# Two attention layers on eight cores: row sums by VectorE transposes, bf16 shift, and a first projection stage in four banks

## The reference

```python
qkv = x @ Wqkv.T + b          # first block: 16 query heads, ONE key head and ONE value head of 128
attn = softmax(causal(q k^T / sqrt(128)));  ctx = attn @ v
x = layernorm(x + ctx @ Wout.T + bo)
# second block: 16 heads, each with its own query, key and value, from x @ (Wa * column scale);
# causal attention inside each sequence, then ctx @ Wp
x = layernorm(x + attention2(x))
```

## Time and profile before

| | us |
|---|---|
| median of 3 runs (2007.41 to 2011.96) | 2007.47 |
| the profiled execution, its own time | 2012.48 |
| its span, on core 4, the slowest | 2010.7 |
| spans of the eight cores | 2000.0 to 2010.7 |

### The profile page before, as it was taken

How to read it: one execution, slowest core, us unless ns; L and a number is a source line. 1 busy time by engine, 2 the same in 40 slices (tenths; PEclk the granted TensorE clock), 3 DMA queues, 4 the chain that set the end, 5 groups by cost and what they waited for, 6 DMA issues and landing times.

```text
span 2010.7 us, 31172 instructions; the slowest of 8 cores (2000.0 to 2010.7 us)
## 1 busy us (share of the span) xinstructions
PE 1941.8 (97%) x10704; PEld 1032.5 (51%) x10704; DVE 1097.6 (55%) x1872; ACT 1002.4 (50%) x1395; POOL 242.1 (12%) x354
## 2 busy tenths in 40 slices
PE   5999999999999999999999999999999999899997
PEld 3455455545444444645647465564745647444443
DVE  0088889988953554134555545555555555543433
ACT  0288888888843433144454544545354453532221
POOL 1011111111132441000010000001000000100000
PEclk9999999999999999999999999999999999999999
DMA  9511221221486996132121322212131210393752
GB/s 156 108 33 43 53 59 39 62 50 36 89 169 126 277 262 168 32 53 48 33 53 27 64 43 53 44 37 52 29 64 43 53 37 13 63 213 109 221 186 84
DMA packets 87577, 170.11 MB, mean 85 GB/s; under 512 B 38160, under 2 KB 54912, under 8 KB 77440
## 3 DMA queue, kind: packets, MB, share of 16 engines
q0 software_dynamic: 26304, 59.77, 18.7%
q1 hardware_dynamic: 60976, 107.83, 17.8%
q10 hardware_dynamic: 144, 0.52, 0.1%
HBM read 185.69 MB, written 33.80 MB: 109 GB/s over the span
## 4 chain that ended last, share of the span: by engine, by line
PE 89%; DMA 5%; DVE 2%; ACT 2%; issue 1%; POOL 0%; DVEq 0%; ACTq 0%; POOLq 0%; SPq 0%
PE pj L303 33%; PE c_ps L609 11%; PE s_ps L418 11%; PE s_ps L841 10%; PE pj L1039 10%; PE pj L841 5%; PE l_ps L530 3%; PE c_ps L841 3%; DMA bufB<-wo 2%; PE l_ps L841 2%; DMA bufB<-xT 2%; ACT pt L430 1%; PE pj L383 1%; PE pj L759 1%; PE pj L397 0%
## 5 line engine op out<-in xcount | busy, mean ns | idle before, releaser
L430 ACT ACTIVATE pt<-s_ps,mbias 128x1024 bf16<-128x1024 f32 (+2 forms) x640 | 631.2, 989 | 458.6 <-PE s_ps L418 357.8
L303 PE MATMUL pj<-bufA,ws 128*128 128x512 bf16 x2048 | 480.5, 379 | 2.6 <-DVE ws L965 1.7
L609 PE MATMUL c_ps<-pt,v 128*128 128x512 bf16 (+3 forms) x1280 | 342.3, 349 | 9.2 <-ACT cf L622 8.2
L303 PEld LDWEIGHTS pj<-bufA,ws 128*128 128x128 bf16 x2048 | 198.5, 98 | 232.1 <-issue 5.6
L487 DVE TENSOR_TENSOR acc<-acc,pt 128x1024 f32<-128x1024 f32 x180 | 220.1, 1223 | 123.1 <-ACT pt L430 119.3
L303 PE MATMUL pj<-bufB,ws 128*128 128x512 bf16 x1024 | 275.5, 382 | 1.2 <-DVE mhat L387 0.7
L1039 PE MATMUL pj<-wv,bufA 128*128 128x256 bf16 x2048 | 238.9, 273 | 1.7 <-DVE mbias L400 1.0
L438 POOL TENSOR_SCALAR_AFFINE_SELECT pt<-pt 128x256 bf16<-128x256 bf16 x256 | 123.0, 482 | 905.1 <-ACT pt L430 890.7
L1039 PEld LDWEIGHTS pj<-wv,bufA 128*128 128x128 bf16 x2048 | 199.7, 98 | 39.2 <-issue 2.3
L869 ACT ACTIVATE sqs<-z 128x512 f32<-128x512 f32 x128 | 80.6, 629 | 240.2 <-DVE z L864 231.6
L609 PEld LDWEIGHTS c_ps<-pt,v 128*128 128x128 bf16 x1280 | 124.7, 98 | 144.4 <-issue 21.8
(11 more groups left out here) (113 smaller groups left out, 1879.8 us busy)
## 6 DMA issues: line engine op xcount, KB each, us to landing
rb<-rr_res SPq DMA_DIRECT2D x116, 256.0 KB, 3.5
ws<-wqk POOLq DMA_DIRECT2D x32, 512.0 KB, 5.2
z<-x SPq DMA_DIRECT2D x16, 1024.0 KB, 6.6
x_res<-z SPq DMA_DIRECT2D x16, 1024.0 KB, 6.9
z<-x_res SPq DMA_DIRECT2D x16, 1024.0 KB, 6.6
out<-z SPq DMA_DIRECT2D x15, 1024.0 KB, 8.6
ws<-wq POOLq DMA_DIRECT2D x16, 512.0 KB, 5.6
bufB<-wo POOLq DMA_DIRECT2D x4, 2048.0 KB, 26.5
```

The lines of the kernel that those rows point to most:

```text
L303: tok = P.pe(lambda t, c=c, b=b: t.matmul(pj[b][:, :], lhs(c), rhs(c), start=(c == 0), stop=(c == NCH - 1)), waits=wt, inc=(c == NCH - 1))
L430: self.exp_tok[g] = P.ac(lambda s: s.activation(pt[:, 0:n], sp[:, 0:n], AF.Exp, bias=mbias[h % 2][:, :]), waits=[self.s_tok[g], self.mb_ok ...
L609: last = t.matmul(c_ps[:, q0:q0 + n], self.vbuf(h)[:, c * 128:(c + 1) * 128], pt[:, o:o + n], start=(beg and n_ == 0), stop=(end and n_ == 1))
```

## The change

Three parts.

1. **First projections.** Keys and values of window 0 are computed together, chunk by chunk as xT arrives, then both queries; windows 1 and 2 send each chunk through four chains in four banks (keys, values, queries of heads 0 and 1), and window 3 through three, with the fourth behind it, around `stats(0)`. Values are computed like keys (features on the partitions, 16 matmuls of 512 columns, with a bias for each partition), and four matmuls with the identity (`turn_v`) turn each window. Windows 1 to 3 arrive in four transfers each, and `wv1`, `ws[0]` and `ws[1]` are loaded earlier. Keys are moved out of PSUM by DVE.
2. **Shift.** `mhat` and the identity are bf16, in both attentions.
3. **Row sums of attention 2.** `turn` transposes the folded 128x512 sums in blocks of 32x32 on DVE and reduces each block's rows: 16 numbers for each partition and window. After window 3, `lsum_turned` splits the 128x64 numbers in two bf16 tiles, both on DVE, and two matmuls of 32 columns with `quads` finish the sum. `recip` inverts 64x32 and stores rows of 128 bytes. `split_hi` is gone. The steps are 0, 4, 10, 18 for `turn`, 19 for `lsum_turned`, 2, 4, 6, 8 for the reads and 4, 6, 8, 10 for the norms.

```diff
-    mhat = [const(f"mhat{i}", [128, 1], F32) for i in range(2)]
-    identf = const("identf", [128, 128], F32)
+    mhat = [const(f"mhat{i}", [128, 1], BF16) for i in range(2)]
+    ident = const("ident", [128, 128], BF16)
+    quads = const("quads", [128, 32], BF16)
+    l4 = const("l4", [128, 64], F32)
+    l4hi = const("l4hi", [128, 64], BF16)
+    l4lo = const("l4lo", [128, 64], BF16)
...
-    hi2 = [row("hi2", 40960, 512, BF16)]
-    lo2 = [row("lo2", 41984, 512, BF16)]
+    tr2 = row("tr2", 40960, 512, F32)
...
     tok_wk = P.dma("gpsimd", "lwk", wk1[:, :], wq_d[16, :, :])
+    tok_wv = P.dma("gpsimd", "lwv", wv1[:, :], wq_d[17, :, :])
     load_x(0, 4)
-    tok_wv = P.dma("gpsimd", "lwv", wv1[:, :], wq_d[17, :, :])
     ws_tok = [None] * 3
-    ws_tok[0] = P.dma("gpsimd", "ws0", ws[0][:, :], wq_d[0, :, :])
-    load_x(1, 2)
-    ws_tok[1] = P.dma("gpsimd", "ws1", ws[1][:, :], wq_d[1, :, :])
-    load_x(2, 2)
-    load_x(3, 2)
+    for i in (0, 1):
+        ws_tok[i] = P.dma("gpsimd", f"ws{i}", ws[i][:, :], wq_d[i, :, :])
+    load_x(1, 4)
+    load_x(2, 4)
+    load_x(3, 4)
     ws_tok[2] = P.dma("gpsimd", "ws2", ws[2][:, :], wq_d[2, :, :])
...
+    tok_quads = None
+    for q in range(4):
+        tok_quads = P.ve(lambda v, q=q: v.tensor_copy(quads[32 * q:32 * q + 32, :],
+                                                      ident[32 * q:32 * q + 32,
+                                                            32 * q:32 * q + 32]),
+                         waits=[tok_ident])
...
+        def turn(self, w):
+            src, n = self.sources(w)
+            tr = self.turned
+            t = P.ve(lambda v: v.transpose(tr[:, :], src), waits=[self.fold_ok[w], self.turn_ok])
+            self.src_read[n] = t
+            self.turn_ok = P.ve(lambda v: v.reduce_sum(
+                l4[:, 16 * w:16 * w + 16], tr[:, :].rearrange("p (b k) -> p b k", k=32),
+                axis=AX.X), waits=[t, self.l4_ok])
+        def lsum_turned(self, h):
+            t1 = P.ve(lambda v: v.tensor_copy(l4hi[:, :], l4[:, :]),
+                      waits=[self.turn_ok, self.hl_free[0]])
+            t2 = P.ve(lambda v: v.tensor_sub(l4lo[:, :], l4[:, :], l4hi[:, :]), waits=[t1])
+            self.l4_ok = t2
+            def mm(t):
+                t.matmul(l_ps[0:64, 0:32], l4hi[:, :], quads[:, :], start=True, stop=False)
+                return t.matmul(l_ps[0:64, 0:32], l4lo[:, :], quads[:, :], start=False, stop=True)
+            self.l_tok[h] = P.pe(mm, waits=[t2, tok_quads, self.r_tok.get(h - 1), bank_free[7]])
+            self.hl_free[0] = self.l_tok[h]
...
         def recip(self, h):
+            if self.turned:
+                self.r_tok[h] = P.ve(lambda v: v.reciprocal(self.r4[0:64, 0:32],
+                                                            l_ps[0:64, 0:32]),
+                                     waits=[self.l_tok[h], self.ro_tok.get(h - 1)])
+                self.ro_tok[h] = P.dma(
+                    "sync", f"{self.tag}ro",
+                    rr_d[self.row0 + h, :, :].rearrange("w (b c) -> (w b) c", c=32),
+                    self.r4[0:64, 0:32], waits=[self.r_tok[h]])
+                return
...
                     put(g0 + self.split_at[w], "split", h, w)
-                    put(g0 + self.l_at[w], "lsum", h, w)
+                    if self.turned is None or w == NW - 1:
+                        put(g0 + self.l_at[w], "lsum", h, w)
...
-                if not self.fold_out and g + 1 < n:
+                early = self.fold_out or self.turned
+                if not early and g + 1 < n:
+                    self.sums(g + 1)
+                for what, hh, w in todo:
+                    if what == "split" and not self.turned:
+                        self.split_hi(w)
+                if early and g + 1 < n:
                     self.sums(g + 1)
                 for what, hh, w in todo:
                     if what == "split":
-                        self.split_hi(w)
-                if self.fold_out and g + 1 < n:
-                    self.sums(g + 1)
-                for what, hh, w in todo:
-                    if what == "split":
-                        self.split_lo(w)
+                        (self.turn if self.turned else self.split_lo)(w)
...
-                    if what == "lsum":
+                    if what == "lsum" and not self.turned:
                         self.lsum(hh, w)
+                    elif what == "lsum":
+                        self.lsum_turned(hh)
...
+    vt = [pt1[w // 2][:, w % 2 * 512:(w % 2 + 1) * 512] for w in range(NW)]
+    sets = [[pj[0][:, :], pj[1][:, :], s_ps[0][:, 0:512], s_ps[0][:, 512:1024]],
+            [c_ps[:, :], l_ps[:, :], s_ps[1][:, 0:512], s_ps[1][:, 512:1024]]]
+    set_free = [[None] * 4, [None] * 4]
+    start_w = [(wk1, tok_wk), (wv1, tok_wv), (ws[0], ws_tok[0]), (ws[1], ws_tok[1])]
+    vt_ok = {}
+    def start_mm(w, kind, c):
+        wt, tw = start_w[kind]
+        b = sets[w % 2][kind]
+        return P.pe(lambda t: t.matmul(b, wt[:, c * 128:(c + 1) * 128], xt(c, w),
+                                       start=(c == 0), stop=(c == NCH - 1)),
+                    waits=[tw, tok_x[(w, c)]] + ([set_free[w % 2][kind]] if c == 0 else []),
+                    inc=(c == NCH - 1))
...
+    def start_kinds(w, kinds, hook=None):
+        for c in range(NCH):
+            for kind in kinds:
+                tok = start_mm(w, kind, c)
+                if c == NCH - 1:
+                    start_evac(w, kind, tok)
+            if c == 3 and hook is not None:
+                hook()
...
+    def turn_v(w):
+        b = sets[w % 2][1]
+        def mm(t):
+            last = None
+            for j in range(4):
+                last = t.matmul(b[:, j * 128:(j + 1) * 128], vt[w][:, j * 128:(j + 1) * 128],
+                                ident[:, :], start=True, stop=True)
+            return last
+        t = P.pe(mm, waits=[vt_ok[w], tok_ident])
+        at1.first_pt = [t]
+        t = P.ve(lambda v: v.tensor_copy(v1[:, w * 512:(w + 1) * 512], b), waits=[t])
...
-    kv_end = [None]
-    for w in range(NW):
-        run(k1_group(w))
-        v1_group(w)
-        run(q1_group(0, w))
-        if w == NW - 1:
-            kv_end[0] = P.tok("mm")
-            at1.stats(0)
-        if w > 0:
-            run(q1_group(1, w - 1))
+        set_free[w % 2][1] = t
+    start_kinds(0, (0, 1))
+    start_kinds(0, (2,))
+    start_kinds(0, (3,))
+    start_kinds(1, (0, 1, 2, 3), lambda: turn_v(0))
+    start_kinds(2, (0, 1, 2, 3), lambda: turn_v(1))
+    start_kinds(3, (0, 2, 1), lambda: turn_v(2))
+    kv_end = [P.tok("mm")]
+    load_ws(3, wq_d[3, :, :], kv_end[0])
+    pj_free[0], pj_free[1] = set_free[0][0], set_free[0][1]
+    for i in range(4):
+        bank_free[2 + i] = set_free[i // 2][2 + i % 2]
+    bank_free[6] = set_free[1][0]
+    for c in range(8):
+        start_mm(3, 3, c)
+    at1.stats(0)
+    for c in range(8, NCH):
+        last = start_mm(3, 3, c)
+    turn_v(3)
     at1.shift(0)
-    run(q1_group(1, NW - 1))
+    start_evac(3, 3, last)
+    load_ws(4, wq_d[4, :, :], last)
+    bank_free[5] = set_free[1][3]
+    bank_free[7] = set_free[1][1]
...
-              acc2, f2, False, hi2, lo2, cf2, rb2, rl2, r42, (1, 5, 11, 19), (4, 6, 12, 20), 1,
-              (3, 5, 7, 9), (5, 7, 9, 11))
+              acc2, f2, False, [], [], cf2, rb2, rl2, r42, (0, 4, 10, 18), (0, 0, 0, 19), 1,
+              (2, 4, 6, 8), (4, 6, 8, 10), tr2)```

VectorE at the end of an even head of attention 2, from the last sums of window 3 on; `acc` is the sum, `l` the table `l4`. Before:

```order
L495 TENSOR_TENSOR acc_124<-acc_124,pt_3_123 128x256 [waits gp,ve]
L497 TENSOR_TENSOR acc_124<-acc_124,pt_3_123 128x128
L502 TENSOR_TENSOR acc_124<-acc_124 128x512 [waits ve]
L400 TENSOR_REDUCE mbias_57<-pj 128x1 [waits mm]
L462 CAST acc_124<-pt_0_120 128x512 [waits gp,ve]
L465 TENSOR_TENSOR acc_124<-acc_124,pt_0_120 128x384 [waits ve]
L515 TENSOR_TENSOR lo_126<-acc_124,hi_125 128x512 [waits ac]
```

More of the change, by code:

```diff
@@ L139, in build_program @@
     bqk_d = nc.dram_tensor("bqk", [128, 18], F32, kind="ExternalInput")
-    bv_d = nc.dram_tensor("bv", [128, 128], F32, kind="ExternalInput")
     wo_d = nc.dram_tensor("wo", [4, H, 128, 512], F32, kind="ExternalInput")
@@ L397, in shift @@
             tm = P.pe(lambda t: t.matmul(pj[b][:, 0:128], mhat[e][:, :].broadcast_to([128, 128]),
-                                         identf[:, :], start=True, stop=True),
+                                         ident[:, :], start=True, stop=True),
                       waits=[self.mh_ok[h], tok_ident, pj_free[b]])
@@ L745, in evac, with start_evac @@
+    def start_evac(w, kind, tok):
+        b = sets[w % 2][kind]
+        sl = slice(w * 512, (w + 1) * 512)
+        if kind == 0:
+            t = P.ve(lambda v: v.tensor_scalar(kT[:, sl], b, bqk[:, 16:17], None, op0=ALU.add),
+                     waits=[tok] + tok_small)
             for h in range(H):
                 at1.k_ok[(h, w)] = t
-            return t
```

(33 more changed lines are left out.)

21 lines of the change are left out of this document (8 added, 13 removed).

## The result

The changed kernel takes 2015.97 us (median of 7 runs, 2014.56 to 2017.47), the kernel before 2008.97 beside it. The ratio is 1.0035, its 95% interval 1.0023 to 1.0047: slower, by about as much as can be told from nothing. 2018 had been predicted, a rise of 10.5 us on 2007.47; the medians rise by 7.0. In the traces TensorE is busy for 25 us less (1941.8 to 1916.7) and the span is 5 us longer (2010.7 to 2015.9), so some 30 us of new waiting and lower clock have to be found. Lines are now those of the changed kernel.

What follows compares the result with a forecast made beforehand. TensorE, busy 1941.8 of 2010.7 us, was taken as the bound. Work terms of -40.2 and waits and clock of +50.7 made net +10.5 us: 2023 for the profiled execution, 2018 on the median; range 1975 to 2036.

Steps and rivals of the forecast that it cites:

- start: First projections: attention 1's first scores come at 78.8 us instead of 91.70, -12.9 us.
- 60 groups of L530: Attention 2's row sums: 60 groups of four matmuls at 0.44 us each leave TensorE, -26.4 us.
- even ends, 7: Ends of heads 0 to 12 in attention 2: TensorE waits 3.4 us each for shift and split, +23.8 us.
- head 14: End of the last even head, without a projection stream, where TensorE waits anyway: put at +2 us.
- odd ends, 7: Ends of odd heads in attention 2: TensorE waits 1.6 us each for the split, +11.2 us.
- step 10, 7: Odd heads: turn and norm ahead of the shift's reduction; new wait less the old 0.57 us, 0.5 each, +3.5 us.
- clock: Attention 2's even ends: waits bring the lower clock at six of seven, 1.7 us each, +10.2 us.
- The shift in attention 2: The bf16 shift's saving there lies ahead of waits and is lost in them; costed at nothing.
- The second: Rival: short waits in attention 2, a turn as fast as the cast, no lower clock; 1994 us, chance 0.15.
- the third: Rival: float32 transpose takes twice an addition, longer waits, clock falls at odd ends too; 2046 us, chance 0.12.
- The fourth: Rival: the start gains nothing, xT arrives later or window 0 keeps the clock low; 2028 us, chance 0.08.
- The first: Rival: attention 2's split is ready when TensorE comes, so the work alone counts, -40.2; 1961 us, chance 0.2.

Runs made afterwards that it cites:

- e2: Only the new first projections against the kernel before; shift in float32 and attention 2's row sums as before: 1998.16 us, ratio 0.9937.
- e1: The changed kernel with attention 2's row sums as before; new start and bf16 shift stay: 1991.30 us, ratio 0.9889.
- e7: The changed kernel with the split right behind the last turn, turns one step later, row sum matmuls at step 21, reciprocal, reads and norms later: 1968.50 us, ratio 0.9789.
- e3: The changed kernel with the table's split (cast and subtraction) directly behind the fourth turn, steps unchanged: 1997.97 us, ratio 0.9931.
- e8: The changed kernel with turns, reads, norms and row sum matmuls one step later, the split still issued with the matmuls: 1989.57 us, ratio 0.9887.
- e5: The changed kernel with each transpose done twice into the same tile, 60 more instructions on VectorE: 2046.37 us, ratio 1.0163.

## Why the prediction was right

The mechanism holds: the work of TensorE that goes is lost again in waits behind the turn and behind the split, and in the clock. The size is less exact than it looks. The 2018 is 2 us too high, but the rise is 7.0 us and not 10.5, since the kernel before had a median of 2008.97 beside the changed one and not of 2007.47; between the profiled executions it is 5.0 (2012.5 to 2017.5), against which the sum was made. "Measured" in the table is of the profiled executions.

| term | predicted, us | measured, us | from |
|---|---|---|---|
| start | -12.9 | -12.7 to -13.8 | e2's median, first scores 77.87 |
| shift, attention 1 | -2.6 | about -2 | attention 1's end, e1 against e2, on cores whose clock stayed up |
| 60 groups of L530 | -26.4 | -26.4 | 0.44 each; e7's stretch fits it |
| 15 pairs of 32 columns | +1.7 | +2.1 | 15 x 0.14 |
| even ends, 7 | +23.8 | +22.5 | 7 x (1.36 + 1.86) |
| head 14 | +2 | about 0 | 4.09 ahead of L547; it was 3.96 ahead of L530 |
| odd ends, 7 | +11.2 | +10.0 | L547: 27.1 - 4.1 - 7 x 1.86 |
| step 10, 7 | +3.5 | +4.7 | 8.8 at L1126, less the 4.1 that L407 no longer waits for values (4.3 in e1, 0.2 here) |
| clock | +10.2 | +9.6 on core 4 | 2.7 + 4 x 1.7 |

**The turn.** The transpose was the one operation without a row. It was taken like an addition, 0.69, and takes 0.711; the reduction was put on the slope at 0.69 and takes 0.686. Behind the warning of the Trainium skill (VectorE: DVE Perf Modes, Rules for kernel authors) that a reduction is "the slowest DVE op" nothing shows here: 0.686 against 0.692 for the addition of the same width. From the start of the fold to the start of the shift's reduction it was 0.61 us and is 2.22 now, 1.61 more, where 1.6 had been worked out. Cast and subtraction of 64 columns were put at their upper bound of 0.28 and take 0.19 and 0.23, which is most of what the even and odd ends are short of the forecast.

Two groups of this kernel (line, count, ns min/median/max, first and last start):

```profile
L533 DVE STREAM_TRANSPOSE tr<-acc x60: 711/711/716, 853.2 to 1749.2; 128x512 f32<-128x512 f32 x60
L535 DVE TENSOR_REDUCE l<-tr x60: 685/686/689, 854.0 to 1750.0; 128x16 f32<-128x512 f32 x60
```

**Which terms were mis-sized, and cancel.** Head 14 was given 2 us and has none: TensorE waits 4.09 us there, and waited about 4 before. The even and odd ends together were put 2.5 us too high. Step 10 was put 1.2 too low: the wait of 0.57 ahead of the shift did go, but the new one is 1.25 and not the 1.1 that would have made it 0.5. Inside an even end the waits were to be about 1 and 2 us or more; they are 1.36 and 1.86.

And two things are in none of the terms. From 855 us to the last shift TensorE's idle time is 4.3 us in e1 and 41.5 in the changed kernel, +37.2; ahead of that it is the same. With -24.6 for 56 groups, +2.0 for the pairs and +9.6 for the clock that is +24.2, while 29.0 lie between the two stretches on core 4 (959.9 and 930.9). Of the 4.8 us between, 1.7 are a fall of the clock at 837.0 us in the changed kernel's trace, ahead of attention 2, which core 4 of e1 doesn't have and cores 1 and 5 of it do. Most of the rest is the 0.16 us by which a wait's idle time is counted short, as read at 1147.28 above: 22 more waits than in e1 make 3.5 of it, the same size as the 3.1 that are left.

That the total still comes out low has causes outside the change. From the end of attention 1 to the second projections the profiled core of the kernel before takes 241.8 us and that of the changed kernel 237.1: TensorE waited 2.23 us for the output weights in the one trace, and the clock fell there (at 624.9 us). Two other cores of the kernel before take 237.2. And attention 1 has two falls of the clock in the one trace and one in the other. By stages of the two traces: -13.8 up to the first scores, -2.6 in attention 1 (1.7 of it that fall), -4.7 up to the second projections, +26.4 from there to the last shift (2.6 less than against e1, which already has the shift in bf16), and -0.1 to the end. That is +5.2, as the spans say.

**The shift in attention 2.** It was costed at nothing, since "the same saving lies ahead of waits and is lost in them". Without the new waits it is worth 3.1 us (e2 to e1). With them TensorE waits for L410 at every shift, as the rows above show, and comes to it sooner for nothing.

**The clock.** The forecast had six falls of seven even ends, by rows of other stages at 2.22 and 1.66 us. Core 4 has a double stretch at one end, single ones at four and none at two, though the waits are the same 1.36 + 1.86 at all of them; that six times 1.7 is so near to the 9.6 is luck. e3's single waits of 1.99 us bring it at all seven even ends on core 3 (on the other cores at three to seven), and e8's of 1.28 at none. Nor do the two rows that the forecast leaned on hold each time. In attention 1 of the changed kernel TensorE also waits once for 2.22 us (to 530.18), and the granted clock of that stretch is 1.00 (524 to 534 us). And at 837.0 us it falls behind two waits of 0.93 and 0.68 us, where the kernel before had the same two and stayed at 1.00.

**The rivals.** The second (a turn as fast as a cast) fell with the transpose's 0.711 us; the third (slower, by the transpose's price) was built as e5, whose two transposes take 1.42 us, and gave the 2046 that had been worked out. Its parts are 18.4 us of waits where 14.7 had been put, and 12.8 of clock where it had 13.6; but the clock falls longer at the even ends, and at two of the odd ends only. The fourth fell with e2. The first, "the waits are covered", is what e7 does. The work alone had been put at -40.2, and e7 is 42.3 under the kernel before (1968.50 against 2010.82). The step from "VectorE is half idle" to "so it is covered" is what the changed kernel got wrong, and the order is all that differs.
